# A tile-routed MetaFormer block on one core: image adds on neighbouring floats, an earlier block load, and a last image pair that comes and goes in seven pieces

## Chip, cores, metric

One Trainium2 chip, one core. The metric is the device time of the program in microseconds (us); a kernel's time is the median of several runs.

## What is computed

`x` is 32 images of 64 channels and 56 x 56 points, fp32. A convolution block with signs for weights and inputs gives a new `x`; then every point is a token of 64 channels that goes through the one of eight experts which a gate picks (at most 15,680 tokens per expert, the rest get 0). Cut to that:

```
x = x + conv_block(layernorm_over_channels(x))
t = x as tokens (image, point, channel)
h = layernorm(t)
e = argmax(softmax(h @ gate_w + gate_b));  p = its probability
y = relu(h @ w1[e] + b1[e]) @ w2[e] + b2[e]     # times p, 0 for tokens beyond the capacity
out = (t + y) back as images
```

## The kernel before

The images are worked in 16 pairs (two images of 64 channels fill the 128 partitions; a pair is 3136 columns). The program has two halves, with one instruction stream for each engine and semaphores between them.

*First half* (to about 960 us). Each pair goes through the convolution block. SyncE stores the result by pieces into `block_output` in DRAM. The tokens, two at a time (the same point of both images), are transposed, normalised and routed, and POOL scatters them as rows into `pairs_by_group` (L511, out of the SBUF buffer `ROWS`, whose two halves belong to even and odd pairs). Rows with the same two experts lie in the same blocks of 256 rows; a block is called a super tile, or tile here, and there are 231.

*Second half.* A pass `super_pass(k)` stands in the code of TensorE, ScalarE, VectorE and POOL for each tile k:

- SyncE loads the tile's rows (`load_rows`, L621) and the weights of its experts (`load_weights` L625, or `early_weights` L633 for tiles 0 to 47) into a ring of 12. The number of the weights is read out of SBUF (`kinds`, or `early_kinds` by way of `order`), which SyncE does with register loads.
- TensorE transposes the rows (L869), applies the first layer (L878), the second (L888), and transposes the result of an earlier tile back (L896).
- ScalarE and VectorE empty the PSUM banks; VectorE's share is L1394 (a quarter of the first layer's outputs) and L1407 to L1416 (the gate's factor, and values that aren't finite).
- POOL scatters the results, two indirect DMAs per tile (L543), into `results_by_pair`, where each row is a token pair in the order of the images.

*Images put together.* When the results of a pair are back, SyncE loads its tokens (`load3`, L664) into `T3` and the pair's block out of `block_output` (`load_block`, L570) into `RX`, which is the buffer `ROWS` used again: even pairs at column 0, odd pairs at column 3136. A pair is seven groups. For each, TensorE transposes four pieces of tokens (`image_group`, L908, 112 tokens x 128 channels each), and VectorE adds the bank to the block in `RX` (`add_group`, L1423, 128 x 448). Then SyncE stores the pair to `out` (`store3`, L672). The groups stand behind the passes 62 + 12 n + 5 to 11 for pair n, so seven passes of twelve carry one. Pairs 14 and 15 come after the last pass, when no pass is left to carry them.

`T3` holds 28 tokens per partition on 112 partitions. Before, partition p has the tokens 28 p to 28 p + 27, so that group g's bank has every 28th token's column: the add goes over `RX` in steps of 28 floats:

```
done_v = done_pairs.rearrange("(n p j) c -> n p j c", p=PP, j=PJ)
part = RX[:, odd * HW:odd * HW + HW].rearrange("p (t j) -> p j t", j=PJ)[:, g * GROUP:(g + 1) * GROUP, :]
```

*SyncE's order of work.* After the first half it issues 12 tiles' weights, then (after all scatters but those of the last odd pair) 12 tiles' rows, then waits for the last odd pair's scatters (L660). Tiles 12 to 47 follow (`early_tile`), each when the result of the tile 12 before it is out of the ring. Before tile 24 stand the load of `kinds` (L688, 231 single numbers, for the tiles from 48 on) and the block of pair 0, before tile 36 the block of pair 1. From tile 63 on, loads of tokens and blocks and stores of pairs stand between the tiles (`two_pairs`). At the end: tokens and block of pair 14, store of pair 13, wait for every scatter, tokens of pair 15, its block (which waits for the store of pair 13, whose buffer it takes), and both stores.

Of the kernel before, what the change touches and what calls it, by code (L numbers as in the profile page):

```python
# [14 lines left out]
def metaformer_kernel(nc, x, move1, w3, g1, be1, mu1, va1, pm1, ps1, pb1, move2, w_pw,  # L15
# [4 lines left out]
    ds = bass.ds  # L20
# [88 lines left out]
    done_v = done_pairs.rearrange("(n p j) c -> n p j c", p=PP, j=PJ)  # L109

    ctx = ExitStack()
    with ctx:
# [212 lines left out]
        s_out = [sem("out_even_stored"), sem("out_odd_stored")]  # L325

# [68 lines left out]
        def hidden(q):  # L395

            return (bank[2][:, 0:SUPER], bank[3][:, 0:SUPER], bank[2][:, SUPER:2 * SUPER], bank[4][:, 0:SUPER])[q]

# [154 lines left out]
        def _(sp):  # L553
# [12 lines left out]
            def load_block(q, odd):  # L566
                if isinstance(q, int) and q == 0:
                    for j in range(NCH):
                        sp.wait_ge(s_x2s[j], 16 * PAIRS)
                sp.dma_start(RX[:, odd * HW:odd * HW + HW], x2d[ds(q, 1)].rearrange("a p m -> (a p) m")).then_inc(s_rx[odd], 16)  # L570
# [86 lines left out]
            for u in range(RING):  # L657
                load_rows(placed(u), u)
            for g in range(NG):
                sp.wait_ge(s_sc[1][g], 16 * scatters[g] * (PAIRS // 2))  # L660
# [14 lines left out]
            def two_pairs(i, first=False):  # L675
                for r in range(SIDE):
                    k = LOAD_AT + r
                    super_tile(i * SIDE + k, k % RING, i * (SIDE // RING) + k // RING)
                    for odd in range(2):
                        if r == odd * STRIDE + LOAD_FROM:  # L680
                            load3(i * 2 + odd, odd)
                            if not first:
                                reload(i * 2 + odd, odd)
                        if (r - STORE_AFTER - odd * STRIDE) % SIDE == 0 and not (first and r < STORE_AFTER):
                            store3(i * 2 + odd if r >= STORE_AFTER + odd * STRIDE else i * 2 + odd - 2, odd)
            for k in range(RING, EARLY):
                if k == 2 * RING:
                    sp.dma_start(kinds[:, :], first_rows[0, KIND:KIND + 1, :], allow_slow_non_contiguous=True).then_inc(s_kind, 16)  # L688
                if k in (2 * RING, 3 * RING):
                    load_block(k // RING - 2, k // RING - 2)  # L690
# [9 lines left out]
            reload(q, 0)  # L700
            store3(q - 1, 1)
            for u in range(RING):
                sp.wait_ge(s_back[u], 16 * SUB * len(range(u, NSUP, RING)))
            load3(q + 1, 1)
            reload(q + 1, 1)
            store3(q, 0)
            store3(q + 1, 1)
            for k in range(2):
                sp.wait_ge(s_out[k], 16 * PAIRS // 2)
# [3 lines left out]
        def _(pe):  # L713
# [188 lines left out]
            def image_group(q, odd, g):  # L902
                if g == 0:
                    wait(pe, s_in3[odd], (q - odd) * 8 + 16)
# [27 lines left out]
        def _(act):  # L932
# [120 lines left out]
            super_pass(NSUP + 2, (NSUP + 2) % RING, t=False, h=False, y=False)  # L1053


        @block.vector
        def _(dve):
# [360 lines left out]
            def add_group(q, odd, g):  # L1418
# [3 lines left out]
                part = RX[:, odd * HW:odd * HW + HW].rearrange("p (t j) -> p j t", j=PJ)[:, g * GROUP:(g + 1) * GROUP, :]  # L1422
                V.scalar_tensor_tensor(out=part, in0=image_bank(odd, g)[:, 0:GROUP * PP].rearrange("p (j t) -> p j t", t=PP),  # L1423
# [44 lines left out]
```

## Time and profile before

| | |
|---|---|
| three runs | 1753.56, 1764.42, 1766.09 us; median 1764.42 |
| the profiled execution | 1770.21 us |
| its span (first to last instruction) | 1768.4 us |
| busy in the span | TensorE 88%, VectorE 83%, ScalarE 70%, POOL 59% |
| DMA | 351.8 MB, mean 199 GB/s |

Durations are read from the profiled execution, so a sum is made against its span. Times of a row count from the start of the span. An instruction's busy time can overlap the next one's start on the same engine.

### The profile page before, as it was taken

How to read it: one execution, taken by the hardware profiler on the slowest of the kernel's cores; microseconds unless marked ns; L12 is line 12 of the kernel's file. 1: busy time of each engine (PE TensorE's matmuls, PEld its weight loads, DVE VectorE, ACT ScalarE, POOL GpSimd, SP SyncE). 2: the span in 40 equal slices, each digit the busy share in tenths (PEclk: the TensorE clock that was granted, in tenths of full speed). 3: DMA queues.
4: the chain of work that ended last, by engine and by line, in shares of the span. 5: the costliest groups of instructions: out<-in, count | busy, mean ns of one | idle time of the engine just before them, and what ended most of it. 6: DMA issues, size and time to landing. Idle time of an engine off the chain costs nothing.

```text
span 1768.4 us, 40163 instructions
## 1 busy us (share of the span) xinstructions
PE 1558.3 (88%) x10344; PEld 843.0 (48%) x10344; DVE 1473.5 (83%) x3653; ACT 1233.8 (70%) x4066; POOL 1051.0 (59%) x1054
## 2 busy tenths in 40 slices
PE   7998889889898888977762989999999999999994
PEld 2344444334343344434441555566666666666662
DVE  4588888978889888887885778889999999999995
ACT  4788786877778787776751767777666676666661
POOL 3115666656676666855677766666655666666562
PEclk9999988989999999997875999999999999999996
DMA  9546878675567574644335577888999999998995
GB/s 241 89 109 136 176 160 174 150 165 149 123 156 172 133 133 109 165 104 113 88 103 164 156 221 223 243 233 251 296 293 318 304 308 292 311 304 277 300 303 209
DMA packets 302288, 351.80 MB, mean 199 GB/s; under 512 B 48516, under 2 KB 252516, under 8 KB 296004
## 3 DMA queue, kind: packets, MB, share of 16 engines
q1 hardware_dynamic: 260708, 264.23, 56.7%
q0 software_dynamic: 41120, 85.81, 16.1%
q14 instruction: 106, 0.87, 0.2%
q8 instruction: 34, 0.56, 0.1%
q10 hardware_dynamic: 320, 0.33, 0.1%
HBM read 179.70 MB, written 180.01 MB: 203 GB/s over the span
## 4 chain that ended last, share of the span: by engine, by line
PE 50%; DVE 21%; issue 13%; ACT 6%; POOL 6%; DMA 3%; SPq 1%; ACTq 0%; POOLq 0%; DVEq 0%
PE bank L878 10%; PE bank L888 10%; PE bank L869 5%; PE bank L779 5%; PE bank L896 3%; POOL pairs_by_group L511 3%; PE bank L838 3%; PE bank L741 3%; DVE ROWS L1423 3%; PE bank L789 3%; PE bank L812 2%; POOL X L505 2%; DVE N L1414 1%; DVE X L1394 1%; ACT SQR L1013 1%
## 5 line engine op out<-in xcount | busy, mean ns | idle before, releaser
L511 POOL DMA_INDIRECT pairs_by_group<-ROWS,idx x400 | 432.3, 1081 | 119.5 <-issue 113.5
L543 POOL DMA_INDIRECT results_by_pair<-X,PAIRNO x310 | 308.9, 996 | 187.2 <-PE bank L869 92.4
L1033 ACT ACTIVATE X<-bank,X 128x256 f32<-128x256 f32 x693 | 283.5, 471 | 61.0 <-PE bank L878 61.0
L505 POOL TENSOR_TENSOR X<-Z,X 128x448 f32 (+1 forms) x112 | 140.8, 1257 | 267.2 <-DVE Z L1367 250.0
L878 PE MATMUL bank<-X 64*128 64x256 f32 x1848 | 264.9, 405 | 9.1 <-DVE X L1394 5.6
L888 PE MATMUL bank<-X 128*64 128x256 f32 x1848 | 251.4, 393 | 1.0 <-DVE X L1394 1.0
L779 PE MATMUL bank<-S,WB 128*128 128x448 bf16 x1008 | 229.6, 376 | 0.0
L543 POOL DMA_INDIRECT results_by_pair<-S,PAIRNO x152 | 153.2, 1008 | 97.3 <-PE bank L869 69.2
L1026 ACT ACTIVATE X<-bank 128x256 f32<-128x256 f32 x231 | 88.5, 383 | 161.7 <-PE bank L869 161.0
L878 PEld LDWEIGHTS bank<-X 64*128 64x128 f32 x1848 | 163.8, 187 | 59.6 <-issue 46.9
L869 PE MATMUL bank<-ident,X 128*64 128x128 f32 x1848 | 153.7, 288 | 22.8 <-DMA X<-pairs_by_group 17.5
L1013 ACT ACTIVATE SQR<-bank 128x64 f32<-128x64 f32 (+1 forms) x800 | 167.8, 256 | 0.0
L779 PEld LDWEIGHTS bank<-S,WB 128*128 128x128 bf16 x1008 | 95.7, 102 | 151.3 <-issue 71.3
L1013 ACT ACTIVATION_READ_ACCUMULATOR SQR<-bank 128x1 f32 (+1 forms) x800 | 166.3, 244 | 0.0
L888 PEld LDWEIGHTS bank<-X 128*64 128x64 f32 x1848 | 112.5, 136 | 111.6 <-issue 78.4
L741 PE MATMUL bank<-X,row_weights 128*128 (+1 forms) x224 | 124.8, 644 | 31.1 <-ACT SQ L961 22.3
L808 PE MATMUL bank<-biasrow,ones 65*128 65x432 bf16 x144 | 52.0, 361 | 102.0 <-POOL X L505 50.4
L812 PE MATMUL bank<-row_weights,X 128*128 128x144 f32 x800 | 137.9, 314 | 0.0
L970 ACT ACTIVATE N<-Z,cst 128x448 f32 (+1 forms) x112 | 76.7, 685 | 84.1 <-DVE Z L1323 82.9
L812 PEld LDWEIGHTS bank<-row_weights,X 128*128 128x128 f32 x800 | 131.6, 213 | 5.0
L1394 DVE TENSOR_SCALAR X<-bank,X 128x256 f32<-128x256 f32 x231 | 110.7, 479 | 26.5 <-PE bank L878 25.9
L1407 DVE TENSOR_TENSOR N<-bank,X 128x256 f32<-128x256 f32 x231 | 97.4, 422 | 38.1 <-PE bank L896 37.0
(231 smaller groups left out, 3048.7 us busy)
## 6 DMA issues: line engine op xcount, KB each, us to landing
X<-weights_by_group SPq DMA_DIRECT2D x231, 258.5 KB
X<-pairs_by_group SPq DMA_DIRECT2D x231, 134.0 KB
pairs_by_group<-PAD SPq DMA_DIRECT2D x15, 1742.0 KB, 21.8
X<-in_x_dram SPq DMA_DIRECT2D x16, 1568.0 KB
block_output<-X SPq DMA_DIRECT2D x112, 224.0 KB, 2.1
ROWS<-block_output SPq DMA_DIRECT2D x16, 1568.0 KB
Z<-results_by_pair SPq DMA_DIRECT2D x16, 1568.0 KB, 9.6
out_dram<-ROWS SPq DMA_DIRECT2D x16, 1568.0 KB
```

The source lines that it names most:

```text
L505: pool.tensor_tensor(X2[:, j * CW:(j + 1) * CW], Z[:, p.z(j * CW)], X[:, p.x(j * CW, CW)], ALU.add).then_inc(s_x2, 1)
L511: pool.indirect_dma_start(rows, bass.IndirectOffsetOnAxis(ap=idx[0:m, p.odd, k:k + 1], axis=0), ROWS[0:m, p.odd, k, :], None).then_inc(s_s ...
L543: pool.indirect_dma_start(done, bass.IndirectOffsetOnAxis(ap=PAIRNO[:, u, j:j + 1], axis=0), RES[u][:, j, :], None,).then_inc(s_back[u], 16)
L741: mm(centered(c, alone)[:, 0:CW], center[:, :], X[:, cen.x(c * CW, CW)], start=True, stop=True).then_inc(s_cen, 1)
L779: last = mm(CONV[(con.odd + c) % 2][:, 0:CW], WB[:, t, :], S1[:, con.odd, c * CHUNK_ROWS + dy:(c + 1) * CHUNK_ROWS + dy, dx:dx + W], start ...
L812: last = mm(ROWP[g][:, at:at + GW], X2[:, k * P:(k + 1) * P], row_weights[:, :], start=False, stop=k == group_tiles[g][-1])
L869: last = mm(PT[h * C:h * C + C, d * P:(d + 1) * P], RTH[:, u, d, h, 0:C], ident[:, :], start=True, stop=True)
L878: mm(hidden(q), WR[b, ring, q // 2 * P:(q // 2 + 1) * P], XT[b, ring % 2, :], start=True, stop=True).then_inc(s_h, 1)
L888: last = mm(YT[h * C:h * C + C, 0:SUPER], WR[:, b, at:at + C], HB[:, b % 2, q, :], start=q < 2, stop=q >= HC - 2)
L1013: last = A(SQR[0:m, (odd * NG + g) % 2, i, h * C:h * C + C], src[0:m, i, h * C:h * C + C], ACT.Square, accum_out=SSQ[0:m, odd, k:k + 1])
L1033: last = A(HB[:, ring % 2, q, :], hidden(q), ACT.Relu, bias=WR[:, ring, at:at + 1])
L1394: V.tensor_scalar(HB[:, ring % 2, q, :], hidden(q), WR[:, ring, at:at + 1], 0.0, ALU.add, ALU.max).then_inc(s_hb, 1)
```

## The change

Four edits. (1) The tokens' layout in `T3` is turned: partition p now holds the tokens p, p + 112, p + 224, and so on, so that group g covers the columns 448 g to 448 g + 447 of the image, next to each other, and `add_group` works on a plain slice. (2) Pair 0's block is loaded right after the rows of the first twelve tiles; pair 1's block at the place where later odd pairs have theirs; the kinds before tile 36 instead of 24. (3) Pair 15's block goes to a third place in `RX` (`image_at`), so that its load waits for nothing, and its tokens are loaded in seven pieces with a semaphore each; TensorE waits for a piece at a time. (4) The stores of pairs 14 and 15 are issued by ScalarE, seven pieces each, each after its add.

```diff
-    done_v = done_pairs.rearrange("(n p j) c -> n p j c", p=PP, j=PJ)
+    done_v = done_pairs.rearrange("(n j p) c -> n p j c", p=PP, j=PJ)
...
+        s_last = [sem(f"last_tokens_loaded_{g}") for g in range(NG3)]
...
+        def image_at(q):
+
+            return 2 * HW if q == PAIRS - 1 else q % 2 * HW
...
-                sp.dma_start(RX[:, odd * HW:odd * HW + HW], x2d[ds(q, 1)].rearrange("a p m -> (a p) m")).then_inc(s_rx[odd], 16)
+                at = image_at(q) if isinstance(q, int) else odd * HW
+                sp.dma_start(RX[:, at:at + HW], x2d[ds(q, 1)].rearrange("a p m -> (a p) m")).then_inc(s_rx[odd], 16)
...
             for u in range(RING):
                 load_rows(placed(u), u)
+            assert HW <= TILES * 3 * UNIT
+            load_block(0, 0)
             for g in range(NG):
                 sp.wait_ge(s_sc[1][g], 16 * scatters[g] * (PAIRS // 2))
...
                             load3(i * 2 + odd, odd)
-                            if not first:
+                            if not first or odd:
                                 reload(i * 2 + odd, odd)
...
             for k in range(RING, EARLY):
-                if k == 2 * RING:
+                if k == 3 * RING:
                     sp.dma_start(kinds[:, :], first_rows[0, KIND:KIND + 1, :], allow_slow_non_contiguous=True).then_inc(s_kind, 16)
-                if k in (2 * RING, 3 * RING):
-                    load_block(k // RING - 2, k // RING - 2)
                 early_tile(k, k % RING, k // RING)
...
             load3(q, 0)
             reload(q, 0)
+            load_block(q + 1, 1)
             store3(q - 1, 1)
             for u in range(RING):
                 sp.wait_ge(s_back[u], 16 * SUB * len(range(u, NSUP, RING)))
-            load3(q + 1, 1)
-            reload(q + 1, 1)
-            store3(q, 0)
-            store3(q + 1, 1)
+            last_tokens = done_v[ds(q + 1, 1)].rearrange("a p j c -> (a p) j c")
+            for g in range(NG3):
+                j = slice(g * GROUP, (g + 1) * GROUP)
+                sp.dma_start(T3(1).rearrange("p (j c) -> p j c", c=P)[:, j, :], last_tokens[:, j, :]).then_inc(s_last[g], 16)
             for k in range(2):
-                sp.wait_ge(s_out[k], 16 * PAIRS // 2)
+                sp.wait_ge(s_out[k], 16 * (PAIRS // 2 - 1 + NG3))
...
             def image_group(q, odd, g):
-                if g == 0:
+                if isinstance(q, int) and q == PAIRS - 1:
+                    pe.wait_ge(s_last[g], 16)
+                elif g == 0:
                     wait(pe, s_in3[odd], (q - odd) * 8 + 16)
...
+            for q in range(2 * ROUNDS, PAIRS):
+                for g in range(NG3):
+                    m = slice(g * GROUP * PP, (g + 1) * GROUP * PP)
+                    act.wait_ge(s_c3, q * NG3 + g + 1)
+                    act.dma_start(out_v[q, :, m], RX[:, image_at(q) + m.start:image_at(q) + m.stop]).then_inc(s_out[q % 2], 16)
...
-                part = RX[:, odd * HW:odd * HW + HW].rearrange("p (t j) -> p j t", j=PJ)[:, g * GROUP:(g + 1) * GROUP, :]
-                V.scalar_tensor_tensor(out=part, in0=image_bank(odd, g)[:, 0:GROUP * PP].rearrange("p (j t) -> p j t", t=PP),
+                at = image_at(q) + g * GROUP * PP
+                part = RX[:, at:at + GROUP * PP]
+                V.scalar_tensor_tensor(out=part, in0=image_bank(odd, g)[:, 0:GROUP * PP],
                                        scalar=col(CB), in1=part, op0=ALU.add, op1=ALU.add).then_inc(s_c3, 1)
```

SyncE's order at tile 24, before (the end of tile 23's loads and the rows of tile 24; N is the buffer of the kinds, ROWS that of the blocks, TENSOR_LOAD a register load):

```order
349 L633 DMA X<-weights_by_group 128x517
350 L688 DMA N<-pairs_by_group 1x231x1
351 L570 DMA ROWS<-block_output 128x3136
352 L629 TENSOR_LOAD N
353 L629 ISA x2
354 L621 ISA
355 L621 DMA X<-pairs_by_group 128x2x134
```

The same engine in the changed kernel, where tile 11's rows are issued and tile 12's follow:

```order
217 L627 DMA X<-pairs_by_group 128x2x134
218 L576 DMA ROWS<-block_output 128x3136
219 L635 TENSOR_LOAD N
220 L635 ISA x2
221 L627 ISA
222 L627 DMA X<-pairs_by_group 128x2x134
```

The block of pair 0 has moved from before tile 24 to between the rows of tiles 11 and 12; the kinds stand, in the changed kernel, where the block of pair 1 was, before tile 36.

SyncE's end, before (Z is the buffer of the tokens):

```order
1018 L664 DMA Z<-results_by_pair 112x28x128
1019 L570 DMA ROWS<-block_output 128x3136
1020 L672 DMA out_dram<-ROWS 128x3136
1021 L664 DMA Z<-results_by_pair 112x28x128
1022 L570 DMA ROWS<-block_output 128x3136
1023 L672 DMA out_dram<-ROWS 128x3136 x2
```

and in the changed kernel:

```order
1018 L672 DMA Z<-results_by_pair 112x28x128
1019 L576 DMA ROWS<-block_output 128x3136 x2
1020 L680 DMA out_dram<-ROWS 128x3136
1021 L714 DMA Z<-results_by_pair 112x4x128 x7
1022 L112 UNCONDITIONAL_BRANCH
```

Pair 15's block now stands right behind pair 14's, ahead of pair 13's store; its tokens are seven issues; the stores of pairs 14 and 15 have left the queue. They are the last instructions of ScalarE, after the copies of the last tiles:

```order
874 L1052 ACTIVATE X<-bank,X 128x256
875 L1047 ACTIVATE X<-X 128x2x64
876 L1052 ACTIVATE X<-bank,X 128x256
877 L1047 ACTIVATE X<-X 128x2x64 x2
878 L1067 DMA out_dram<-ROWS 128x448 x14
```

Nothing follows them there but the end of the program.

## Rows read from the trace of the kernel before

**Rows 1.** Busy time by stretch: PE, PEld, DVE, ACT, POOL, granted clock, DMA share, GB/s

```profile
1600.00:1700.00 100.00, 98.01 (x848) 61.18 (x846) 92.07 (x259) 69.07 (x180) 60.79 (x60) 1.00 0.96 307
1742.00:1768.40 26.40, 7.70 (x32) 5.38 (x32) 8.99 (x9) 0.00 (x0) 0.00 (x0) 0.50 0.71 243
```

**Rows 2.** Waits, 1200 to 1700 us: total us, times, longest us

```profile
PE bank L878 <- DVE X L1394: 5.0, 12, 0.7
```

**Rows 3.** Timeline, PE: start us, us, what; each starts one tile's pass

```profile
1178.79 0.66 PE L869 MATMUL bank<-ident,X 128*64 128x128 f32 x8
...
1181.82 0.66 PE L869 MATMUL bank<-ident,X 128*64 128x128 f32 x8
...
1185.24 0.66 PE L869 MATMUL bank<-ident,X 128*64 128x128 f32 x8
...
1722.25 0.66 PE L869 MATMUL bank<-ident,X 128*64 128x128 f32 x8
```

**Rows 4.** Timeline near the end of the passes, image adds and a wait

```profile
1717.81 1.05 DVE L1423 SCALAR_TENSOR_TENSOR ROWS<-bank,cst,ROWS 128x448 f32<-128x448 f32 x1
...
1721.35 1.04 DVE L1423 SCALAR_TENSOR_TENSOR ROWS<-bank,cst,ROWS 128x448 f32<-128x448 f32 x1
...
1726.45 1.13 PE L878 MATMUL bank<-X 64*128 64x256 f32 x8 [0.63 <-DVE X L1394]
```

**Rows 5.** Groups by line and form, DVE: count | busy us, mean ns | idle before

```profile
L1423 DVE SCALAR_TENSOR_TENSOR ROWS<-bank,cst,ROWS 128x448 f32<-128x448 f32 x112 | 117.2, 1051 | 12.1 <-DMA ROWS<-block_output 11.2 <-PE bank L908 0.2
...
L1342 DVE SCALAR_TENSOR_TENSOR Z<-bank,cst,Z 128x448 f32 x70 | 47.3, 676 | 0.7
```

**Rows 6.** Timeline, SP: issues of DMAs in the second half

```profile
1033.78 0.34 SPq L633 DMA_DIRECT2D X<-weights_by_group  x1
1034.16 0.99 SPq L688 DMA_DIRECT2D N<-pairs_by_group  x1
...
1038.78 0.34 SPq L633 DMA_DIRECT2D X<-weights_by_group  x1
...
1113.18 0.34 SPq L633 DMA_DIRECT2D X<-weights_by_group  x1
...
1160.08 4.43 SPq L621 DMA_DIRECT2D X<-pairs_by_group  x1
```

**Rows 7.** Timeline, PE, around the stall before tile 24, and tile 47

```profile
1037.58 0.66 PE L869 MATMUL bank<-ident,X 128*64 128x128 f32 x8
...
1045.95 1.12 PE L869 MATMUL bank<-ident,X 128*64 128x128 f32 x8 [5.26 <-DMA X<-weights_by_group]
1047.00 2.08 PE L878 MATMUL bank<-X 64*128 64x256 f32 x8
...
1051.35 0.66 PE L869 MATMUL bank<-ident,X 128*64 128x128 f32 x8
...
1118.10 0.66 PE L869 MATMUL bank<-ident,X 128*64 128x128 f32 x8
```

**Rows 8.** Timeline, the tail

```profile
1732.70 1.08 POOL L543 DMA_INDIRECT results_by_pair<-X,PAIRNO  x1 [1.24 <-ACT X L1038]
...
1742.40 0.62 SPq L664 DMA_DIRECT2D Z<-results_by_pair  x1
...
1747.41 15.71 SPq L672 DMA_DIRECT2D out_dram<-ROWS  x2
...
1751.74 1.75 PE L908 MATMUL bank<-ident,Z 112*128 112x112 f32 x8 [8.67 <-DMA Z<-results_by_pair]
1755.31 7.45 DVE L1423 SCALAR_TENSOR_TENSOR ROWS<-bank,cst,ROWS 128x448 f32<-128x448 f32 x7 [11.18 <-DMA ROWS<-block_output]
```

**Rows 9.** SyncE's own waits, 960 to 1000 us: total us, times, longest us

```profile
SPq L660 <- DMA pairs_by_group<-ROWS,idx: 14.1, 4, 5.1
```

**Rows 10.** Line L586, stores of 224 KB to `block_output`

```profile
DMA to landing us min/median/max: 1.9/2.1/10.1
```

## The prediction

> **What bounds the kernel now.** I read the busy table by stretches first. From 1200 to 1700 us the second half (weights applied tile by tile, images put together beside it) has TensorE busy 98 us of 100 with its clock granted in full; from 1742 us to the end it is busy 7.7 of 26.4 us at a granted clock of 0.50, the lower of its two levels (1.2 of 2.4 GHz) [rows 1]. So there are three things to look for: the 2% that TensorE does not work in the long stretch, the tail, and the start of the second half. The waits say who causes the 2%: TensorE's first layer (L878) waits for VectorE's L1394 [rows 2]. The timeline shows the beat. A pass of one tile without image work takes 1181.82 - 1178.79 = 3.03 us, one with an image group 1185.24 - 1181.82 = 3.42 us [rows 3]: both are TensorE's own work. VectorE's pass with an image group takes 1721.35 - 1717.81 = 3.54 us [rows 4], 0.1 us more than TensorE's. Over the seven such passes of a pair VectorE falls behind by 0.7 us, and TensorE pays it at the end of the seven; the row at 1726.45 is such a wait, 0.63 us [rows 4]. The sum over the stretch: the tile transposed at 1181.82 is number 68, the one at 1722.25 number 230 [rows 3], 162 passes in 540.4 us. 97 of them carry an image group (13 whole pairs of seven, and six of the 14th), 65 don't: 97 x 3.42 + 65 x 3.034 = 529.0. So 11.5 us are lost to VectorE's lag.
>
> The costly instruction in VectorE's pass is the image add L1423: 1051 ns, though L1342, of the same form (448 floats per partition, one PSUM and one SBUF operand, result in place), takes 676 ns [rows 5]. The difference between them is the address step: L1423 reads and writes the image at every 28th float.
>
> At the start of the second half SyncE is the narrow place. A tile's weights are issued every (1113.18 - 1038.78) / 23 = 3.235 us (tiles 24 to 47) [rows 6], while TensorE needs a tile every 3.03 us. Tile 24 comes late: the loads of kinds and of pair 0's block stand ahead of it, 1038.78 - 1033.78 = 5.0 us after tile 23 instead of 3.235, and its landing shares the engines with 1.57 MB. TensorE idles 5.26 us and then works at half speed for a tile (L878 takes 2.08 us, not 1.13). From tile 23's transposes to tile 25's it is 1051.35 - 1037.58 = 13.8 us for two passes worth 6.1: 7.7 us lost [rows 7].
>
> In the tail the last pair's tokens are issued at 1742.40 and are with TensorE at 1751.74; the adds start at 1755.31, when the block has landed, end 7.45 us later, and the store then takes until 1768.4 [rows 8].
>
> **The change part by part.** Durations are of the profiled execution, span 1768.4 us in 1770.2; the median of the three timed runs is 1764.4, 0.3% lower (they lie from 1753.6 to 1766.1). I take the gains off the median as they stand.
>
> *Image adds on neighbouring floats (112 of them).* The new add has L1342's form: 676 ns [rows 5]. Bounds: 1051 ns (the step is not the reason), and 0.6 us, a little under L1342. I take 676, the row with the same operands. VectorE's pass falls by 0.375 to about 3.17 us, under TensorE's 3.42, so the lag doesn't build up; for that a cut of 0.12 us would do. What is late next is TensorE itself, at 3.42. Gain: the 11.5 us. On the reason for the slow add the Trainium skill (SBUF — State Buffer, Door 1: The DMA port swizzle) says that SBUF serves accesses to one 16-byte line at full rate and charges each step to a new line; by it the 375 ns would be this charge and would go whole, and if a step cost nothing, none of it. The trace shows the two durations, not their reason, and the sum would be 28 us by the one and 16.5 by the other.
>
> *The token layout* only changes which tokens a partition holds: as many pieces of 512 B per load, now read 112 rows apart instead of one after the other. No row shows such a read. Bounds: the same 9.3 us (1742.40 to 1751.74) [rows 8], or several times that; I take the same, since the results were scattered row by row by POOL anyway, and keep the other end as a rival.
>
> *Pair 0's block after the first twelve rows.* SyncE waits there 14.1 us for the last scatters (L660) [rows 9], so the issue costs nothing, and its 1.57 MB are through before tile 12 is asked for. If they held up the scatters' landing, SyncE's whole chain would slip by up to their own time, some 5 us; I take 0, since each scatter is small and spaced by POOL. *Pair 1's block* goes to the place where every later odd pair's is: no wait for a DMA shows there. *Kinds before tile 36*: 0.99 us of issue, some 1.25 with the gap, as now before tile 24 [rows 6]; wanted only at tile 48.
>
> Without the stop at tile 24 the weights come every 3.235 us, TensorE eats its lead (tile 23's weights are issued at 1033.78 and used at 1037.58 [rows 6, 7], so landing takes at most 3.8 us, and at least the 2.1 of a 224 KB store [rows 10]; I take 2.7) and, at 0.2 us per tile, from about tile 28 follows SyncE's beat. Tile 47's weights are issued at 1033.78 + 24 x 3.235 - 0.4 (pair 1's block gone) + 1.25 (kinds) = 1112.3; with 2.7 us more TensorE has it at 1115.0, now at 1118.10 [rows 7]. Gain 3.1 us, not 7.7: the stall is mostly exchanged for a steady 0.2 us per tile. Bounds: 7.7 (all of it gone), and -2 (the kinds make a stall with a half-speed tile, as now, or the scatters slip). After tile 48 SyncE is faster and the lead returns.
>
> *The tail.* Pair 15's block is loaded at about 1713 into its own buffer, beside nothing that is urgent, so the wait of the adds until 1755.31 goes. What is late next is the tokens. The first piece (224 KB) can land about 3 us after issue (a store of that size takes 2.1 [rows 10]); SyncE issues the seven some 0.6 us apart. The last piece lands no earlier than the whole load does now, about 9.3 us after the first issue. TensorE's four transposes at half clock take 1.0 us per piece (eight took 1.75 [rows 8]), an add 0.7: both keep up with pieces that come 0.8 to 1.0 us apart. So from the issue: 9.3 + 1.0 + 0.7 + 0.2 (semaphores) + 2.1 (last store [rows 10]) + 0.5 = 13.8 us instead of 1768.4 - 1742.4 = 26.0. Gain 12.2; bounds 9 (pieces a third slower, stores of pair 14 in between) and 15 (last piece after 7 us). ScalarE has nothing queued behind its fourteen stores. With VectorE not behind, POOL's wait of 1.24 us for the last results at 1732.70 [rows 8] goes too: 1.2 us, bounds 0 and 1.8.
>
> **Sum:** 11.5 + 3.1 + 12.2 + 1.2 = 28.0 us. Span about 1740; median 1764.4 - 28.0 = 1736.4 us, 1.6% less.
>
> **Rivals.**
> *A, the add stays at about 1.05 us* (the image buffer or the PSUM bank is slow, not the step). For it: the trace has no add on this buffer at step one. Then VectorE still lags, 11.5 + 1.2 are not won: 1749.
> *B, the pieces follow one another.* The Trainium skill (DMA: Bandwidth & Descriptors, Rules for kernel authors and Anatomy of one DMA) advises against cutting a transfer up and gives about 2 us fixed per DMA; by its fit, as an estimate, seven pieces end to end would need 17.7 us and one load 5.7. As a mechanism of this kernel: if each piece waited for the one before, at about 3 us each, the last would land 21 us after the issue, the tail would take 25.5 us and its 12.2 would be lost but for half a microsecond: 1748. Against it: in 1600 to 1700 us, a pass of 3.2 us holds two loads and two scatters, each of about 2 us or more to land, so DMAs overlap here, at 307 GB/s [rows 1].
> *C, the start gets worse:* the early block holds up the scatters, or the kinds cause a stall at tile 36 as they do at 24 now. 2 to 5 us lost instead of 3.1 won: 1742 to 1745.
> *D, slower than before: the token reads 112 rows apart are slow.* The sixteen token loads stand in SyncE's queue ahead of the tiles' loads; the row load after the first of them was held 4.43 us, to 1164.51 [rows 6], for a tile used at 1181.82 [rows 3]. With its weights' issue and landing (some 7 us) 10 us remain. So from about twice today's 9.3 us TensorE waits, once per pair. At three times it would wait 8.6 us in 15 pairs: 129 us, some 1865 in all; the 28 us are eaten from about 21 us per load. Against it: nothing in the trace but that scattered rows are written at a good rate.
>
> **How the numbers follow.** Forecast 0.74, A 0.05, B 0.07, C 0.10, D 0.04. A measurement here tells about 1% (1746.8 to 1782) from no change. Forecast, C and small change of A and B lie below 1746.8: faster 0.85; A and B same: 0.11; D slower 0.04. The range: the upper end takes in A, B and C with 2 or 3 us of scatter, 1752; the lower end the gain 7.7 + 11.5 + 15 + 1.8 = 36 and some 4 us of scatter (the three runs differ by 12), 1724.
>
> **What would show it.** L1423's successor at about 680 ns; VectorE no longer a releaser of L878; passes of 3.03 and 3.42 us through to the end of each pair; no idle of 5 us before tile 24, but small waits for weights at tiles 28 to 47, and tile 47 some 3 us earlier; the SyncE wait for the last scatters still ending when it does; seven token pieces landing under 1.2 us apart and some 14 us from their first issue to the end. I am wrong if the add is over 0.95 us, if token loads take over 15 us, or if the stretch before tile 48 gets longer.

## The result, and the profile after

The changed kernel takes 1736.0 us (median of four runs, 1731.6 to 1741.9), the kernel before 1765.3 (four runs, 1753.6 to 1766.4). The ratio is 0.9863, 95% interval 0.983 to 0.9896: 18 to 30 us less. The forecast was 1736.4.

The profiled execution after took 1731.6 us, span 1729.8. That is 38.6 us less than the span before, more than the change can have done, so the spans are taken apart first. The marks are the first transposes of tiles 0, 47, 68 and 230 on TensorE, the issue of the last pair's tokens, and the end. Starts are read from the timeline, differences are worked out.

| stretch, us | before | after | less | forecast |
|---|---|---|---|---|
| first half, to tile 0 | 968.2 | 956.0 | 12.2 | 0 |
| tile 0 to 47 | 149.88 | 148.04 | 1.84 | 3.1 |
| tile 47 to 68 | 63.72 | 63.72 | 0 | 0 |
| tile 68 to 230 | 540.43 | 529.08 | 11.35 | 11.5 |
| tile 230 to the tokens' issue | 20.14 | 19.30 | 0.84 | 1.2 |
| tokens' issue to the end | 26.01 | 13.72 | 12.29 | 12.2 |
| sum from tile 0 | 800.2 | 773.9 | 26.3 | 28.0 |

The first half is untouched by the change up to tile 0: the first DMA that stands elsewhere, pair 0's block, is issued 12.8 us after tile 0's first transpose (the row at 968.72 below). The experiments show that this half varies from run to run. The rest, 26.3 us, lies inside the interval.

The image add after, all its instructions (line, form, count: ns minimum/median/maximum, first and last start):

```profile
L1438 DVE SCALAR_TENSOR_TENSOR ROWS<-bank,cst,ROWS x112: 670/677/684, 1173.2 to 1726.7; 128x448 f32<-128x448 f32 x112
```

It was 1051 ns [rows 5], and is now what L1342 takes. Busy time by stretch after (columns as in [rows 1]):

```profile
1040.00:1080.00 40.00, 36.38 (x310) 21.44 (x306) 30.59 (x96) 26.84 (x72) 23.16 (x24) 1.00 0.64 175
...
1200.00:1300.00 100.00, 100.00 (x874) 62.41 (x872) 88.16 (x264) 70.89 (x184) 60.11 (x62) 1.00 0.93 300
...
1705.00:1729.80 24.80, 12.44 (x58) 9.02 (x58) 14.38 (x30) 1.29 (x4) 6.94 (x7) 0.56 0.84 275
```

TensorE now has no idle time at all in the steady stretch (100.00 of 100, not 98), and VectorE, at 88, waits for TensorE. The waits of 1200 to 1680 us have no row any more in which L885 (before: L878) waits for VectorE; VectorE's own wait for the transposes back has grown:

```profile
DVE N L1421 <- PE bank L903: 34.6, 142, 0.4
ACT X L1042 <- PE bank L885: 29.3, 147, 0.3
PEld bank L885 <- issue: 25.2, 147, 0.2
```

where the kernel before had, from 1200 to 1700 us,

```profile
DVE N L1407 <- PE bank L896: 19.6, 62, 0.4
```

TensorE's timeline, a start of each tile's pass (L876 is the transpose of the rows): the first of the second half, around the kinds at tile 36, tile 47, then 68, 69 and 230; between them SyncE's issue of pair 0's block.

```profile
955.97 1.12 PE L876 MATMUL bank<-ident,X 128*64 128x128 f32 x8 [16.90 <-DMA X<-pairs_by_group]
...
968.72 0.40 SPq L576 DMA_DIRECT2D ROWS<-block_output  x1
...
1063.92 0.66 PE L876 MATMUL bank<-ident,X 128*64 128x128 f32 x8
...
1068.23 0.66 PE L876 MATMUL bank<-ident,X 128*64 128x128 f32 x8 [1.20 <-DMA X<-weights_by_group]
...
1104.01 0.66 PE L876 MATMUL bank<-ident,X 128*64 128x128 f32 x8 [0.16 <-issue]
...
1167.72 0.66 PE L876 MATMUL bank<-ident,X 128*64 128x128 f32 x8
...
1171.14 0.66 PE L876 MATMUL bank<-ident,X 128*64 128x128 f32 x8
...
1696.80 0.66 PE L876 MATMUL bank<-ident,X 128*64 128x128 f32 x8
```

The idle of 5.26 us before tile 24 [rows 7] is gone. In its place stand one of 1.20 us at tile 36, behind the kinds, and many of about 0.2 us: TensorE follows SyncE's beat. From 1167.72 to 1696.80 it is 529.08 us for the 162 passes that were worked out as 529.0 of TensorE's own work.

The tail after: the stores of both pairs by ScalarE, the seven token pieces, TensorE's transposes and the last add.

```profile
1711.00 16.77 ACTq L1067 DMA_DIRECT2D out_dram<-ROWS  x14
...
1716.11 3.90 SPq L714 DMA_DIRECT2D Z<-results_by_pair  x7
...
1719.12 1.01 PE L917 MATMUL bank<-ident,Z 112*128 112x112 f32 x4 [3.52 <-DMA Z<-results_by_pair]
1720.69 1.01 PE L917 MATMUL bank<-ident,Z 112*128 112x112 f32 x4 [0.56 <-DMA Z<-results_by_pair]
1721.96 4.71 PE L917 MATMUL bank<-ident,Z 112*128 112x112 f32 x20 [0.27 <-DMA Z<-results_by_pair]
...
1726.71 0.68 DVE L1438 SCALAR_TENSOR_TENSOR ROWS<-bank,cst,ROWS 128x448 f32<-128x448 f32 x1 [0.18 <-PE bank L917]
```

The first piece is with TensorE 3.0 us after its issue, and the transposes of the last five run without a pause, at half clock (granted clock 0.56 over this stretch; four took 1.01 us, against 0.55 in the steady stretch). The last add ends at 1727.4, the program 2.4 us later. The end of its chain of waits (start us, us, what) shows the last scatter's landing and the last groups' transposes:

```profile
1712.95 3.04 DMA results_by_pair<-X,PAIRNO
...
1721.96 2.86 PE bank L917 x12
...
1724.83 1.86 PE bank L917 x8
```

### The profile page after: what moved, and what is told of

Same layout as the page of the kernel before. It is cut to its first block, busy times and chain, and to the rows that moved or that the text cites. A ratio compares the mean times of both kernels' runs of the same rounds, so it can differ in the third digit from the quotient of the medians.

```text
span 1729.8 us, 40181 instructions
## 1 busy us (share of the span) xinstructions
PE 1544.1 (89%) x10344; PEld 836.6 (48%) x10344; DVE 1438.9 (83%) x3653; ACT 1232.6 (71%) x4066; POOL 1051.5 (61%) x1054
## 3 DMA queue, kind: packets, MB, share of 16 engines
q10 hardware_dynamic: 2336, 3.54, 0.6%
## 4 chain that ended last, share of the span: by engine, by line
PE 55%; issue 13%; DVE 10%; POOL 9%; ACT 5%; SPq 4%; DMA 2%; POOLq 0%; ACTq 0%; DVEq 0%
PE bank L885 12%; PE bank L895 11%; PE bank L876 7%; POOL pairs_by_group L516 5%; PE bank L786 4%; PE bank L903 4%; PE bank L748 3%; POOL X L510 3%; PE bank L845 3%; PE bank L917 2%; PE bank L796 2%; PE bank L819 2%; SPq L635 2%; SPq L627 1%; ACT SQR L1022 1%
## 5 line engine op out<-in xcount | busy, mean ns | idle before, releaser
L885 PE MATMUL bank<-X 64*128 64x256 f32 x1848 | 263.9, 404 | 0.0
L548 POOL DMA_INDIRECT results_by_pair<-S,PAIRNO x152 | 149.7, 985 | 94.2 <-PE bank L876 65.3
L885 PEld LDWEIGHTS bank<-X 64*128 64x128 f32 x1848 | 159.9, 187 | 50.5 <-issue 39.7
L876 PE MATMUL bank<-ident,X 128*64 128x128 f32 x1848 | 153.3, 287 | 22.2 <-DMA X<-pairs_by_group 17.5
L748 PE MATMUL bank<-X,row_weights 128*128 (+1 forms) x224 | 122.1, 631 | 29.1 <-ACT SQ L970 20.2
```

The costliest lines, as they stand in the source:

```text
L548: pool.indirect_dma_start(done, bass.IndirectOffsetOnAxis(ap=PAIRNO[:, u, j:j + 1], axis=0), RES[u][:, j, :], None,).then_inc(s_back[u], 16)
L748: mm(centered(c, alone)[:, 0:CW], center[:, :], X[:, cen.x(c * CW, CW)], start=True, stop=True).then_inc(s_cen, 1)
L876: last = mm(PT[h * C:h * C + C, d * P:(d + 1) * P], RTH[:, u, d, h, 0:C], ident[:, :], start=True, stop=True)
L885: mm(hidden(q), WR[b, ring, q // 2 * P:(q // 2 + 1) * P], XT[b, ring % 2, :], start=True, stop=True).then_inc(s_h, 1)
```

## The experiments

Theory: the parts add up, each in its own stretch (the add in the steady stretch, SyncE's beat at the start, order and pieces in the tail). Rivals stand with each run. All the stretches in one table, us:

| kernel | to tile 0 | 0 to 47 | 68 to 230 | 230 to tokens | tokens to end |
|---|---|---|---|---|---|
| before | 968.2 | 149.88 | 540.43 | 20.14 | 26.01 |
| changed | 956.0 | 148.04 | 529.08 | 19.30 | 13.72 |
| p1_add | 956.8 | 149.23 | 529.08 | 19.19 | 24.14 |
| p2_early | 954.6 | 148.68 | 540.47 | 20.15 | 26.13 |
| p3_no_early | 962.5 | 150.25 | 529.08 | 19.38 | 14.22 |
| s1_steps | 966.3 | 148.10 | 529.39 | 19.13 | 14.82 |
| t1_whole_tokens | 952.3 | 148.21 | 529.08 | 19.90 | 18.36 |
| t2_two_buffers | 955.7 | 148.77 | 529.08 | 22.18 | 13.46 |
| t3_whole_stores | 953.0 | 148.06 | 529.08 | 18.62 | 16.65 |
| l1_one_lookup | 957.4 | 142.18 | 529.08 | 19.32 | 14.38 |
| l2_one_lookup_before | 959.2 | 141.22 | 540.08 | 20.14 | 26.27 |
| b1_store14_late | 954.9 | 141.22 | 529.08 | 18.61 | 16.50 |

Tile 47 to 68 is 63.7 in all of them. The kernels s1, t1, t2 and t3 ran once each, so they are read by stretches and rows and not by their total time. How far a single profile can be trusted shows where kernels share the code of a stretch. From tile 68 to 230 they agree within 0.4 us. From tile 230 to the end the same tail took 33.0, 33.6 and 33.7 us (changed, p3, l1). From tile 0 to 47 the old order took 149.2 to 150.3 us (before, p1, p3) and the new one 148.0 to 148.8 (changed, p2, s1, t1, t2, t3). Up to 1.0 us of that is one early pass, from tile 2 to tile 3: it took 4.0 us in the kernel before, changed, p1, p3, s1 and l1, 3.0 to 3.2 in p2, t1, l2 and b1, and 3.9 and 3.7 in t2 and t3. From 3 to 6 us after tile 0's first transpose the granted clock was 0.50 in the kernel before and 0.72 in l2, and the first layer of tile 2 took, in this order:

```profile
974.03 2.08 PE L878 MATMUL bank<-X 64*128 64x256 f32 x8
...
964.99 1.13 PE L880 MATMUL bank<-X 64*128 64x256 f32 x8 [0.39 <-ACT X L1035]
```

**p1_add**, the kernel before with the new layout and add alone:

```diff
-    done_v = done_pairs.rearrange("(n p j) c -> n p j c", p=PP, j=PJ)
+    done_v = done_pairs.rearrange("(n j p) c -> n p j c", p=PP, j=PJ)
...
-                part = RX[:, odd * HW:odd * HW + HW].rearrange("p (t j) -> p j t", j=PJ)[:, g * GROUP:(g + 1) * GROUP, :]
-                V.scalar_tensor_tensor(out=part, in0=image_bank(odd, g)[:, 0:GROUP * PP].rearrange("p (j t) -> p j t", t=PP),
+                at = odd * HW + g * GROUP * PP
+                part = RX[:, at:at + GROUP * PP]
+                V.scalar_tensor_tensor(out=part, in0=image_bank(odd, g)[:, 0:GROUP * PP],
```

> The kernel before with the turned token layout and the add on neighbouring floats alone; loads, order of SyncE and stores as before. Theory (the parts add up, each in its own stretch): the add takes 677 ns, tile 68 to tile 230 takes 529.1 us instead of 540.4 and the tail from the last tokens' issue to the end about 25.3 us instead of 26.0 (seven adds of 0.38 us less, of which TensorE's half-speed transposes keep most); tile 0 to tile 47 stays at 149.9 us. In all 12 to 13 us less than before, ratio 0.993. Rival (the steady stretch gains from the early block or the kinds, which leave the queue freer): tile 68 to 230 stays above 535 us.

Measured 1744.4 us against 1762.9 before, ratio 0.9908 (0.9875 to 0.9941). The group of the add in its profile:

```profile
L1424 DVE SCALAR_TENSOR_TENSOR ROWS<-bank,cst,ROWS 128x448 f32<-128x448 f32 x112 | 75.7, 678 | 14.8 <-DMA ROWS<-block_output 12.1 <-PE bank L908 2.4
```

The add alone brings the steady stretch to 529.08, to the hundredth the changed kernel's, with blocks and kinds at their old places: the rival falls. It also shows that the token reads 112 rows apart cost nothing that the steady stretch feels. The tail fell by 1.9 us, not 0.7.

**p2_early**, the kernel before with blocks and kinds moved alone (the edits of SyncE's early part in the change):

> The kernel before with the loads of blocks and kinds moved alone. Theory (SyncE's beat of 3.2 us per tile sets the start of the second half, so that the stall before tile 24 is mostly exchanged for small waits): no idle of 5 us before tile 24, tile 0 to tile 47 takes 147 to 148.5 us instead of 149.9; tile 68 to 230 stays at 540.4, the tail at 26.0. 1.5 to 3 us less in all, which the timing can't tell from none. Rival 1 (the whole 7.7 us of the stall are won): tile 0 to 47 takes 142 us. Rival 2 (the early block holds up the last scatters): tile 12's rows are issued 2 us or more later after tile 0 than in the kernel before (27.8 us), and tile 0 to 47 gets no shorter.

Measured 1757.5 us, ratio 0.9964 (0.9945 to 0.9982). The waits of its stretch 975 to 1110 us:

```profile
PE bank L869 <- DMA X<-weights_by_group: 5.0, 12, 1.2
```

No idle of 5 us, but twelve waits that sum to 5.0 us; tile 0 to 47 is 1.2 us shorter, a little under what was expected and far from 142. Of this 0.8 us is the pass from tile 2 to tile 3 (3.15 us here, 3.97 before), which the edit doesn't touch, so that 0.4 us are left for the early loads in this profile. The whole program is 3 to 10 us shorter by the ratio, more than that; the later stretches are as before, so by the profiles the rest lies in the first half (under p3). The rows of tile 12 were issued 28.1 us after tile 0; with the block at its old place it was 27.8, 27.8, 29.1 and 27.7 (before, p1, p3, l2). So the early block didn't measurably hold up the scatters, and both rivals fall.

**p3_no_early**, the changed kernel with blocks and kinds at their old places (the same edits undone):

> The changed kernel with the blocks and kinds loaded at their old places. Theory: the stall before tile 24 is back, tile 0 to 47 takes about 149.9 us instead of 148.0, tile 68 to 230 stays at 529.1 and the tail at 13.7 us; 2 us slower than the changed kernel, 24 to 26 us less than before, ratio 0.986. Rival (the first half's 12 us that the changed kernel's profile was shorter by belong to the change): the first half, to tile 0, is 968 us again here and 956 where the early loads are in. Theory for that: the first half varies by some 10 us from run to run with any kernel.

Measured 1740.2 us, ratio 0.9872 (0.9834 to 0.9911). Tile 0 to 47 is 150.25, 2.2 us over the changed kernel, the other stretches as expected; the tail took 14.2, not 13.7. The first half is 962.5 here, 966.3 in s1 and 952 to 957 in the other kernels with the early loads, 956.8 and 959.2 in p1 and l2 without them. It varies by up to 16 us with code that is the same up to tile 0, on both sides, and the 12.2 us by which the changed kernel's profile was shorter there can't be put down to the change. A share of a few us is not excluded by twelve profiles, though none of them shows how loads that are issued after tile 0 would bring it about.

**s1_steps**, seven forms of the add, one per group of a pair. `by(n)` walks a tile at every n-th float, `plain` in order, `aside` is a buffer that nothing else uses then:

```diff
+                if g == 0:
+                    V.scalar_tensor_tensor(**add(part, filled, part)).then_inc(s_c3, 1)
+                if g == 1:
+                    V.scalar_tensor_tensor(**add(by(2), plain(2, filled), by(2))).then_inc(s_c3, 1)
...
+                if g == 4:
+                    V.scalar_tensor_tensor(**add(by(28, aside), plain(28, filled), plain(28))).then_inc(s_c3, 1)
+                if g == 5:
+                    V.scalar_tensor_tensor(**add(plain(28, aside), plain(28, filled), by(28))).then_inc(s_c3, 1)
+                if g == 6:
+                    V.scalar_tensor_tensor(**add(plain(28), by(28, filled), plain(28))).then_inc(s_c3, 1)
```

> The changed kernel with seven forms of the image add, one for each group of a pair: plain; block and result at every 2nd float; every 4th; every 28th; only the result at every 28th; only the block read at every 28th; only the PSUM bank read at every 28th. Groups 1 to 3 put tokens at wrong columns, groups 4 and 5 write beside the image, so those columns are left without the add or in another order. Theory (each step of 16 bytes or more costs, reads or writes alike): 677 ns for plain and for every 2nd float, about 1050 for the 4th and the 28th, and between 677 and 1050 where only one side steps. Rival 1 (any step costs): every 2nd float is at 1050 too. Rival 2 (only the write costs, or only the read): one of the two one-sided forms is at 677, the other at 1050. For PSUM no theory has a number: 677 if the bank's step is free, over 900 if not.

Its groups, 1200 to 1700 us (count | busy us, mean ns). L1450 is plain, L1452 every 2nd float, L1454 every 4th, L1456 every 28th, L1458 only the result stepped, L1460 only the block, L1462 only the PSUM bank:

```profile
L1454 DVE SCALAR_TENSOR_TENSOR ROWS<-bank,cst,ROWS 128x448 f32<-128x448 f32 x13 | 13.7, 1054 | 0.0
L1460 DVE SCALAR_TENSOR_TENSOR SQ<-bank,cst,ROWS 128x448 f32<-128x448 f32 x13 | 13.5, 1038 | 0.0
L1456 DVE SCALAR_TENSOR_TENSOR ROWS<-bank,cst,ROWS 128x448 f32<-128x448 f32 x12 | 12.6, 1047 | 0.0
L1458 DVE SCALAR_TENSOR_TENSOR SQ<-bank,cst,ROWS 128x448 f32<-128x448 f32 x12 | 12.5, 1042 | 0.0
L1462 DVE SCALAR_TENSOR_TENSOR ROWS<-bank,cst,ROWS 128x448 f32<-128x448 f32 x13 | 8.8, 677 | 0.0
L1452 DVE SCALAR_TENSOR_TENSOR ROWS<-bank,cst,ROWS 128x448 f32<-128x448 f32 x13 | 8.8, 677 | 0.0
L1450 DVE SCALAR_TENSOR_TENSOR ROWS<-bank,cst,ROWS 128x448 f32<-128x448 f32 x13 | 8.8, 677 | 0.0
```

So a step of 8 bytes in SBUF is free, a step of 16 bytes costs as much as one of 112, and one stepped side costs as much as both. The Trainium skill (SBUF — State Buffer, Door 1: The DMA port swizzle) says that SBUF has lines of 16 bytes and that it takes two hits in a line to hide the access: at every 2nd float there are two in a line, at every 4th one, and the rows agree. The same note takes 4 floats for a step that is still free; the row at every 4th float (1054 ns) says otherwise, and a step of 3 was not measured. A step in the PSUM bank is free for this instruction. Rival A of the prediction (buffer or bank) is excluded: same buffers, same banks, only the step differs. And four slow adds in a row, of seven, leave the steady stretch at 529.39. By an estimate from the prediction's passes VectorE falls behind by 0.1 us in a slow pass (3.54 against 3.42) and makes up 0.25 in a fast one (3.17), so four would put it some 0.5 us behind. That this much is made up before TensorE has to wait, and the 0.8 of seven is not, would explain the 529.39; it was not traced further.

**t1_whole_tokens**, the changed kernel with the last tokens in one load:

```diff
-            last_tokens = done_v[ds(q + 1, 1)].rearrange("a p j c -> (a p) j c")
-            for g in range(NG3):
-                j = slice(g * GROUP, (g + 1) * GROUP)
-                sp.dma_start(T3(1).rearrange("p (j c) -> p j c", c=P)[:, j, :], last_tokens[:, j, :]).then_inc(s_last[g], 16)
+            load3(q + 1, 1)
...
-                if isinstance(q, int) and q == PAIRS - 1:
-                    pe.wait_ge(s_last[g], 16)
-                elif g == 0:
+                if g == 0:
```

> The changed kernel with the last pair's tokens in one load again; third place for the block and stores in pieces stay. Theory (pieces let transposes and adds run while the rest lands): the load lands 8.5 to 9.3 us after its issue, as the last piece does now, TensorE then has all seven groups before it at half clock, about 0.95 us each, so from the tokens' issue to the end 19 to 20 us instead of 13.7. Rival (a piece has a fixed cost of its own, and a whole load lands sooner): it lands after 6 us or less and the tail is 16.5 us or less.

Its load and its first transposes:

```profile
1713.19 0.33 SPq L672 DMA_DIRECT2D Z<-results_by_pair  x1
1721.95 6.43 PE L912 MATMUL bank<-ident,Z 112*128 112x112 f32 x28 [9.84 <-DMA Z<-results_by_pair]
```

The load lands in 8.8 us, and then 6.4 us of transposes follow: tail 18.36, 4.6 us longer (expected 5.3 to 6.3). The pieces' worth is these transposes, hidden under the landing. The seven issues of the changed kernel:

```profile
L714 SPq DMA_DIRECT2D Z<-results_by_pair x7: 329/509/674, 1716.1 to 1719.5; - x7
...
DMA to landing us min/median/max: 3.0/5.1/5.7
```

TensorE has the first piece 3.0 us after its issue. The last is issued 3.4 us after the first and takes up to 5.7 us, so it lands 9.1 us after the first issue, 0.3 us later than the one load. The Trainium skill (DMA: Bandwidth & Descriptors, Rules for kernel authors) advises one large transfer in place of many small ones; here the seven, of 3.0 to 5.7 us each, overlap, and cutting the load up costs 0.3 us of landing.

**t2_two_buffers**, the changed kernel with the last block in pair 13's place:

```diff
-            return 2 * HW if q == PAIRS - 1 else q % 2 * HW
+            return q % 2 * HW
...
-            load_block(q + 1, 1)
             store3(q - 1, 1)
+            reload(q + 1, 1)
```

> The changed kernel without the third place: the last pair's block goes where pair 13's was, after pair 13's store has landed, but still ahead of the wait for the last scatters. Theory (what counted was that the load stood behind the wait for the scatters in SyncE's order, not the buffer): the block is issued some 6 us after the store of pair 13 and lands before the first token piece; the tail is 13.7 us within 0.7. Rival (the buffer counted): the adds wait for the block again, and the tail is over 16 us.

The tail from the tokens' issue is 13.46, as the theory had it. But the tokens are issued later: tile 230 to the tokens' issue takes 22.18, not 19.30, and neither theory nor rival had that. The chain of waits says why (start us, us, what):

```profile
1710.90 0.97 POOL results_by_pair L548
...
1713.46 5.89 DMA results_by_pair<-X,PAIRNO
...
1719.46 3.63 DMA Z<-results_by_pair
```

The block was issued at 1709.06, and the last scatter needed 5.89 us to land instead of the changed kernel's 3.04. So the third place is worth about 2.6 us (35.64 against 33.02 from tile 230; the same tail as the changed kernel's took up to 33.7), because it lets 1.57 MB pass before the scatters that everything waits for, and not because the adds would wait.

**t3_whole_stores**, the changed kernel with pairs 14 and 15 stored whole by SyncE:

```diff
+            for p in (q, q + 1):
+                sp.wait_ge(s_c3, NG3 * (p + 1))
+                sp.dma_start(out_v[p, :, :], RX[:, image_at(p):image_at(p) + HW]).then_inc(s_out[p % 2], 16)
...
-            for q in range(2 * ROUNDS, PAIRS):
-                for g in range(NG3):
-                    m = slice(g * GROUP * PP, (g + 1) * GROUP * PP)
-                    act.wait_ge(s_c3, q * NG3 + g + 1)
-                    act.dma_start(out_v[q, :, m], RX[:, image_at(q) + m.start:image_at(q) + m.stop]).then_inc(s_out[q % 2], 16)
```

> The changed kernel with pairs 14 and 15 stored whole by SyncE, as before. Theory: the last store begins after the last add and takes 5.6 us to the end, as in the kernel before, instead of 2.4 us for one piece; the tail is 16.5 to 17 us instead of 13.7. Rival (the stores of pair 14 in pieces take the token pieces' bandwidth, so that without them the tokens land sooner): the tail is 15.5 us or less.

```profile
1712.44 3.53 SPq L714 DMA_DIRECT2D Z<-results_by_pair  x7
...
1716.01 7.66 SPq L717 DMA_DIRECT2D out_dram<-ROWS  x2
...
1722.59 0.69 DVE L1436 SCALAR_TENSOR_TENSOR ROWS<-bank,cst,ROWS 128x448 f32<-128x448 f32 x1 [0.30 <-PE bank L920]
```

The tail is 16.65, in the theory's range: the last store takes 5.8 us after the last add. The rival has a grain of truth: without pair 14's stores in the way the tokens are issued 0.7 us sooner (18.62) and the last add ends 10.8 us after the issue instead of 11.3. In sum the stores in pieces are worth 35.27 - 33.02 = 2.2 us, known to about 0.7 like the other parts of the tail.

**l1_one_lookup**, the changed kernel with a tile's place read once:

```diff
-                load_rows(placed(k), u)
-                early_weights(k, u)
+                at = placed(k)
+                load_rows(at, u)
+                group = sp.value_load(early_kinds[0:1, ds(at, 1)].bitcast(i32), min_val=0, max_val=GROUPS - 1)
+                sp.dma_start(WR[:, u], wtab[ds(group, 1)].rearrange("a p w -> (a p) w")).then_inc(s_rt[u], 16)
```

> The changed kernel with one register load less per early tile: the place of a tile, read once for its rows and once more for its weights, is kept in a register. Theory (SyncE's beat of 3.2 us per tile holds TensorE's 3.03 up in tiles 12 to 47, and register loads make the beat): the beat falls by about 1.1 us to some 2.1, no wait for weights is left after tile 12, tile 0 to 47 takes 143 to 144 us instead of 148.0, and about 4.5 us less in all than the changed kernel. Rival 1 (the loads' bandwidth sets the beat): the beat falls by less than 0.3 us and tile 0 to 47 by less than 1.5 us. Rival 2 (the wait for a free place in the ring sets it): the same.

Measured 1729.4 us, ratio to before 0.9823 (0.9796 to 0.985). SyncE's issues at tiles 24 and 25:

```profile
1018.78 0.56 SPq L627 DMA_DIRECT2D X<-pairs_by_group  x1
1020.20 0.35 SPq L646 DMA_DIRECT2D X<-weights_by_group  x1
1021.37 0.56 SPq L627 DMA_DIRECT2D X<-pairs_by_group  x1
1022.79 0.35 SPq L646 DMA_DIRECT2D X<-weights_by_group  x1
```

The beat is 2.59 us here (2.61 over tiles 24 to 35, 3.20 in the changed kernel): a lookup takes 0.6 us, not 1.1. It suffices: the beat is below 3.03, no pass from tile 3 to tile 47 takes over 3.04 us, and tile 0 to 47 is 142.18, 5.9 us less than in the changed kernel, even better than expected. Both rivals fall.

**l2_one_lookup_before**, the same edit in the kernel before:

> The kernel before with one register load less per early tile and nothing else. Theory (SyncE's beat was the cause of the stall before tile 24, the loads in front of it only the occasion): with the beat under TensorE's 3.03 us SyncE is ten us ahead by tile 24, the block and the kinds in front of it cost nothing, no idle over 1 us is left, and tile 0 to 47 takes 142 to 143 us instead of 149.9; in all 7 to 8 us less than before, ratio 0.9955. Rival (the block's 1.57 MB in the queue make the stall, whatever the beat): an idle of 2 us or more before tile 24 stays and tile 0 to 47 takes 145 us or more.

Measured 1752.2 us, ratio 0.9943 (0.9921 to 0.9965); tile 0 to 47 is 141.22 and no pass from tile 2 on takes over 3.04 us, with block and kinds still ahead of tile 24. Of the 8.7 us 1.0 is the pass from tile 2 to tile 3, which varies without the lookup too; the other 7.7 are the whole loss at the stall [rows 7]. So SyncE's beat was the cause of the stall and the loads in front of tile 24 only its occasion; moving them, as the change does, buys 0.4 (p2) to 2.2 us (the changed kernel against p3) where the lookup buys 7.7.

**b1_store14_late**, l1 with pair 14 stored whole behind the token pieces:

```diff
-            for k in range(2):
-                sp.wait_ge(s_out[k], 16 * (PAIRS // 2 - 1 + NG3))
+            store3(q, 0)
+            sp.wait_ge(s_out[0], 16 * PAIRS // 2)
+            sp.wait_ge(s_out[1], 16 * (PAIRS // 2 - 1 + NG3))
...
-            for q in range(2 * ROUNDS, PAIRS):
+            for q in range(PAIRS - 1, PAIRS):
```

> The changed kernel with one register load less per early tile, and pair 14 stored whole by SyncE behind the last token pieces instead of in seven pieces by ScalarE while the last scatters land. Theory (the stores of pair 14 hold up the landing of the last scatters and of the token pieces): from tile 230 to the tokens' issue 18.6 us instead of 19.3, from there to the end 13.2 instead of 13.7 to 14.4; about 1.2 us less than with the early tiles' lookup alone (33.7 us from tile 230 to the end), tile 0 to 47 again about 142.2 us; ratio to before 0.982. Rival (the whole store now competes with the pieces of pair 15 at the very end): tile 230 to the end takes 34 us or more.

Measured 1730.1 us, ratio 0.983 (0.9812 to 0.9847), so no faster than l1. The tokens go out 0.7 us sooner (18.61), as expected, but their issue to the end takes 16.50. The issues of the stores and the last add:

```profile
1711.07 1.09 SPq L682 DMA_DIRECT2D out_dram<-ROWS  x1
...
1712.31 7.63 ACTq L1070 DMA_DIRECT2D out_dram<-ROWS  x7
...
1717.53 0.68 DVE L1441 SCALAR_TENSOR_TENSOR ROWS<-bank,cst,ROWS 128x448 f32<-128x448 f32 x1 [0.26 <-PE bank L920]
```

The last add ends at 1718.2, 10.7 us after the tokens' issue (11.3 in the changed kernel), but the program ends 5.8 us after it, at 1724.0, where it ended 2.4 us after it: the last pieces stand behind the whole store. The rival was right: 35.1 us from tile 230, against 33.7 in l1 and 33.0 in the changed kernel. The best version found is l1_one_lookup.

## Why the prediction was right

*The image add (11.5 us; measured 11.35).* Right in mechanism and size. The add fell to 677 ns where 676 was taken from L1342, VectorE no longer releases L885, and the passes are TensorE's own work; p1 shows that it is this edit alone, s1 that the step is the reason.

*The token layout (no cost).* Right: the steady stretch has no wait for it, and the one load of t1, which reads in the new layout, was with TensorE 8.8 us after its issue, where 9.3 was taken from the old one. Rival D is excluded.

*The tail (12.2 and 1.2; measured 12.29 and 0.84).* Right, and by nearly the steps that were written: the last piece lands 9.1 us after the first issue (9.3 was taken), the last two groups' transposes begin at 8.7, and the end is 13.72 us after it (13.8). One sign that was named is missed: the first pieces reach TensorE 1.6 and 1.3 us apart, not under 1.2. The experiments share the tail out, each part with the others in place: pieces of tokens 4.6 us from the tokens' issue on (18.36 - 13.72), third place 2.6 and stores in pieces 2.2 from tile 230 on. The same tail varied by 0.7 us between profiles, and the 13.72 is the shortest of it (14.22 in p3, 14.38 in l1), so that nearness to a tenth is partly luck. One reason was wrong: the third place was to free the adds from waiting; t2 shows that loading the block ahead of the wait for the scatters does that, and that the third place keeps the block's bytes out of the scatters' way. Rival B, pieces one after another, is excluded by the seven landings (under t1). The fit that it took from the Trainium skill (DMA: Bandwidth & Descriptors, Anatomy of one DMA) is given there for DMAs that POOL issues; SyncE's one load took 8.8 us in t1, not the 5.7 of that estimate.

*The start (3.1 us; measured 1.84, in p2 1.2, or 0.4 without the pass from tile 2 to 3, and 2.2 against p3).* This is the term that was mis-sized. Its mechanism held: the stall before tile 24 was exchanged for SyncE's beat and small waits. The step that failed is "with 2.7 us more TensorE has it at 1115.0": tile 47's weights were issued 144.7 us after tile 0 (forecast 1112.3 - 968.2 = 144.1), and TensorE had the tile 3.3 us later, not 2.7. In the changed kernel that is the row

```profile
1100.69 0.34 SPq L639 DMA_DIRECT2D X<-weights_by_group  x1
```

against 1104.01 on TensorE. The kinds' stall at tile 36 was 1.2 us and brought no half-speed tile: the pass behind it runs at full clock, and the granted clock is 1.00 from 1040 to 1080. Rival C (2 to 5 us lost) is excluded.

*The sum.* 28.0 was forecast, 26.3 measured from tile 0 on. That the median fell on the forecast within half a microsecond owes something to the first half, whose length varies by more than the error of the sum.

## What to carry to other kernels

Where two engines alternate, compare their time per pass, not their shares of the span: 0.1 us per pass on the engine that looks less busy cost 11 us here. A stall with a large transfer in front of it may have its root in the queue that issues: measure the beat of the issues against the beat of the consumer before moving the transfer. At the end of a program, ask of every byte in flight whether it stands ahead of the transfer that the chain waits for.

## What was not expected of the hardware

- With a step of 16 bytes in SBUF this add took VectorE 1054 ns for 448 floats instead of 677, and no more with 112 bytes (1047), nor did it matter whether only the result (1042), only the block (1038) or both were stepped by those 112. A step of 8 bytes was free, and so was one of 112 bytes in PSUM (677).
- The landing of the last indirect scatter took 3.04 us in the changed kernel and 5.89 us in t2, where a load of 1.57 MB was issued shortly before it.
- An idle of 5.26 us on TensorE was followed by a half-speed pass [rows 7]; one of 1.20 us was not.
- The first half took 952 to 968 us in twelve profiles, with the same code up to tile 0. TensorE's busy time varies along with it: up to 950 us it was 786.8 us in t1 (tile 0 at 952.3) and 801.4 us in s1 (966.3), for the same 3890 instructions in the profile. Why TensorE took longer, and whether that is the cause, was not looked into; this stays open.
